# Two-layer network of graph convolutions and feed-forward parts: normalising stages and join unrolled with four slabs in flight, logits by token, weight preparation in stage tails, first scores ahead of the slab product

## What is computed

```python
x = x + _L0_conv_ref(_ln_c(x), ...)          # normalised over the 512 nodes
t = _to_tokens(x)                            # (16, 192, 512)
t = t + _L0_ffn_ref(_ln_t(t), ...)           # 8 experts, 2 for each token
x = _from_tokens(t, x)
x = x + _L1_conv_ref(_ln_c(x), ...)
t = _to_tokens(x)
t = t + _L1_ffn_ref(_ln_t(t), ...)           # quantised, up and down
```

## Time and profile before

| | us |
|---|---|
| median of 3 runs (1862.98 to 1868.24) | 1864.14 |
| the profiled execution's own time | 1862.88 |
| its span | 1861.1 |
| TensorE busy (matmul) | 1435.1 (77%) |
| VectorE busy | 1113.9 (60%) |
| ScalarE busy | 751.4 (40%) |
| GpSimd busy | 635.8 (34%) |

### The profile page before, as it was taken

How to read it: one execution, slowest core, us unless ns; L and a number is a source line. 1 busy time by engine, 2 the same in 40 slices (tenths; PEclk the granted TensorE clock), 3 DMA queues, 4 the chain that set the end, 5 groups by cost and what they waited for, 6 DMA issues and landing times. The chain is left out here.

```text
span 1861.1 us, 28248 instructions
## 1 busy us (share of the span) xinstructions
PE 1435.1 (77%) x8462; PEld 1179.6 (63%) x8462; DVE 1113.9 (60%) x2381; ACT 751.4 (40%) x1181; POOL 635.8 (34%) x918
## 2 busy tenths in 40 slices
PE   4578899999464289999999945497999994277676
PEld 4467788887343278888888834395888883155554
DVE  4622488888465654444445335313788886688886
ACT  2412455555242033333333224222555552177775
POOL 1100065556310446555555421000455565011111
PEclk7778899999697579999999965697999997588988
DMA  6423012221374046556555377343122121112221
GB/s 200 144 82 88 9 60 76 68 68 60 113 229 150 12 121 124 108 97 130 122 120 110 38 200 221 99 113 124 44 76 68 59 76 51 43 51 83 94 76 60
DMA packets 95966, 179.95 MB, mean 97 GB/s; under 512 B 13937, under 2 KB 31905, under 8 KB 95909
## 3 DMA queue, kind: packets, MB, share of 16 engines
q1 hardware_dynamic: 71828, 135.52, 23.1%
q0 software_dynamic: 16384, 31.51, 9.8%
q10 hardware_dynamic: 7696, 12.22, 2.1%
HBM read 113.12 MB, written 66.10 MB: 96 GB/s over the span
## 5 line engine op out<-in xcount | busy, mean ns | idle before, releaser
L731 PE MATMUL g_y<-L_z,L_pt 128*128 128x192 f32 x1024 | 197.5, 337 | 1.5 <-ACT L_pt L944 0.5
L889 POOL TENSOR_TENSOR L_xr<-L_xr,L_lnb 128x192 f32<-128x192 f32 x128 | 106.3, 859 | 208.1 <-DMA L_xr<-x 112.2
L731 PEld LDWEIGHTS g_y<-L_z,L_pt 128*128 128x128 f32 x1024 | 167.4, 194 | 6.8 <-ACT L_pt L944 6.8
L1269 POOL DMA_INDIRECT sums<-x_yo,x_places x64 | 103.0, 1609 | 136.4 <-ACT x_yo L1472 126.3
L936 ACT ACTIVATE L_e<-g_s,L_nm 128x512 f32<-128x512 f32 x128 | 88.0, 687 | 79.2 <-DVE L_nm L777 78.2
L699 PE MATMUL g_z<-L_kw,L_xnT 96*128 96x192 f32 x512 | 97.0, 344 | 26.1 <-DVE L_v L807 26.1
L699 PEld LDWEIGHTS g_z<-L_kw,L_xnT 96*128 96x128 f32 x512 | 87.1, 198 | 38.2 <-DVE L_v L807 38.2
L1381 DVE TENSOR_TENSOR x_mid<-ex_g,x_sig 128x480 f32<-128x480 f32 (+1 forms) x48 | 31.3, 653 | 132.8 <-ACT x_sig L1463 125.5
L896 POOL TENSOR_TENSOR L_t<-L_rstd 128x48 f32<-128x48 f32 x96 | 29.2, 305 | 224.5 <-DVE L_rstd L831 219.5
L777 DVE TENSOR_REDUCE L_nm<-g_s 128x1 f32<-128x512 f32 x128 | 87.5, 684 | 27.6 <-PE g_s L708 26.8
L786 DVE SCALAR_TENSOR_TENSOR L_p<-L_e,L_rl,L_adj 128x512 f32<-128x512 f32 x128 | 99.2, 775 | 4.7 <-DVE L_rl L784 0.3
(11 more groups left out here) (281 smaller groups left out, 3843.8 us busy)
## 6 DMA issues: line engine op xcount, KB each, us to landing
xn_rows<-L_xnT SPq DMA_DIRECT2D x48, 384.0 KB, 3.5
L_xnT<-xn_rows SPq DMA_DIRECT2D x48, 384.0 KB, 3.4
x<-L_y SPq DMA_DIRECT2D x32, 384.0 KB, 2.5
L_xa<-in_x SPq DMA_DIRECT2D x16, 384.0 KB, 3.9
L_raw<-xn_rows SPq DMA_DIRECT2D x16, 384.0 KB, 3.4
L_xr<-in_x SPq DMA_DIRECT2D x16, 384.0 KB, 3.4
L_xa<-x SPq DMA_DIRECT2D x16, 384.0 KB, 3.9
sums<-L_raw ACTq DMA_DIRECT2D x16, 384.0 KB, 3.1
```

The lines of the kernel that those rows point to most:

```text
L731: last = nc.tensor.matmul(out, pt[k % 2][:, P * c:P * c + P], z[q][:, c, :], start=False, stop=(c == NK - 1))
L889: last = nc.gpsimd.tensor_tensor(v_, v_, gain(s.lnb), ALU.add)
L1269: nc.gpsimd.indirect_dma_start(sums, row(places[e % 2][:, 1, t:t + 1]), yo[t % 4][:, :], None, compute_op=ALU.add).then_inc(sent[t % 4], 16)
```

## The change

- **Constants.** The block of constants goes. The identity is the first DMA of n0, then slabs 0 and 1, the other ten constants, slabs 2 and 3, then the 13 weight transfers, all on SP's queue. Only TensorE waits for the identity.
- **normalise** is written out slab by slab. Four slab buffers (xr0 and xr1 join xa), four buffers of normalised rows, three of raw rows; psx is three deep in n0, two deep in n1. Two BN_AGGR replace four of the small steps. In n0 ScalarE instead of VectorE copies the nodes; VectorE's list is shift(b-1), statistics(b). Stores are two DMAs of half a slab.
- **Logits** are made by token: eight products a slab with the nodes as the stationary side, [96, 8] each, kept in one PSUM bank and copied once at the end of n1. `route` loses its transposes and copy, and waits for its tables only ahead of the choice of experts (L1118).
- **conv_weights** becomes the tail of n0 and of the join: VectorE does it behind its last statistics (in the join behind its last copy), TensorE ahead of the last transposes back (n0) or at the end (join); GpSimd clears u and v there, and the clears leave `graph_conv`.
- **combine** is written out too, with three buffers of normalised rows and of node-major slabs; the weight transfers move from ScalarE's queue to SP's, the store of the node-major slab from SP's to ScalarE's.
- **graph_conv**: spread 2 goes ahead of scores 0 of the next slab, transposes 3 behind them, and the slab product behind both; `row_max(b + 1, 0)` goes ahead of `residual` and `variance`; ScalarE's `copy_turned(b, 2)` goes ahead of `row_exp(b, 3)`, and `copy_z` behind `row_exp(b + 1, 0)`.

```diff
--- normalise, SP
+                def load(b):
+                    since(sp, slab_turned, b - 3)
+                    sp.dma_start(xa[b % 4][:, :, :], src[b]).then_inc(xa_in[b % 4], 16)
+                if consts:
+                    consts.first(sp)
+                load(0)
+                load(1)
+                if consts:
+                    consts.rest(sp)
+                load(2)
+                load(3)
+                if prefetch:
+                    prefetch(sp)
+                for b in range(B):
+                    sp.wait_ge(xn_done, b + 1)
+                    for h in range(2):
+                        sp.dma_start(xn_rows[b][:, h, :], xn[b % 4][h]).then_inc(sent[b % 4], 16)
+                    if b + 4 < B:
+                        load(b + 4)
--- normalise, TensorE
+                def logits(b):
+                    pe.wait_ge(nodes_sb, b + 1)
+                    for h in range(2):
+                        at = E * (2 * b + h)
+                        for k in range(NK):
+                            last = nc.tensor.matmul(psl[0:HALF, at:at + E], na[b % 2][:, k, HALF * h:HALF * h + HALF],
+                                                    s.wr[:, k, :], start=(k == 0), stop=(k == NK - 1))
+                    last.then_inc(logits_done, 1)
+                for b in range(D):
+                    turn_slab(b)
+                for b in range(B):
+                    if tail and b == B - 1:
+                        tail.tensor(pe, psx[1])
+                    if route:
+                        if b + D < B:
+                            turn_slab(b + D)
+                        turn_back(b)
+                        since(pe, nodes_sb, b)
+                        if b > 0:
+                            logits(b - 1)
+                    else:
+                        turn_back(b)
+                        if b + D < B:
+                            turn_slab(b + D)
--- normalise, VectorE
+                for b in range(B + 2):
+                    if route and 0 <= b - 2 < B:
+                        copy_nodes(b - 2)
+                    if 0 <= b - 1 < B:
+                        take_shift(b - 1)
+                    if b < B:
+                        statistics(b)
+                if consts:
+                    consts.landed(dve)
+                if tail:
+                    tail.vector(dve, psx[1])
--- normalise, ScalarE
+                for b in range(B + 1):
+                    if route and b < B:
+                        keep_raw(b)
+                    if b < B:
+                        apply_norm(b)
+                    if route and b < B:
+                        send_raw(b)
+                    if not route and b > 0:
+                        copy_nodes(b - 1)
--- ConvWeights
+    def gpsimd(self):
+        for padded in (self.s.u0, self.s.u1, self.s.v0, self.s.v1):
+            self.nc.gpsimd.memset(padded[:, :].bitcast(F32), 0.0)
--- combine, SP and ScalarE
+                for b in range(4):
+                    load(b)
+                prefetch(sp)
+                for b in range(B):
+                    if b + 4 < B:
+                        load(b + 4)
+                    sp.wait_ge(xn_done, b + 1)
+                    for h in range(2):
+                        sp.dma_start(xn_rows[b][:, h, :], xn[b % 3][h]).then_inc(sent[b % 3], 16)
...
+                    act.wait_ge(x_sb, b + 1)
+                    act.dma_start(x_nodes[b], x2[b % 3][:, :, :]).then_inc(kept[b % 3], 16)
--- graph_conv, TensorE
+                    if k == 0:
+                        pe.wait_ge(uv_sb, ready(b))
                     pe.wait_ge(nmax_done, free(n, 2))
...
                         spread(b, q, 1)
+                        spread(b, q, 2)
+                    if project:
+                        scores(b + 1, r, 0)
+                    if softmax:
+                        turn_probs(b, 3)
                     if project:
                         conv_slab(b + 1, r)
-                        scores(b + 1, r, 0)
-                    if softmax:
-                        spread(b, q, 2)
-                        turn_probs(b, 3)
-                    if project:
                         scores(b + 1, r, 1)
--- graph_conv, VectorE
-                for padded in (*u, *v):
-                    nc.vector.memset(padded[:, :].bitcast(F32), 0.0)
...
                         row_probs(b, 3)
+                    if project:
+                        row_max(b + 1, 0)
                     if total:
                         residual(b - 2, q, i - q)
                     if norm:
                         variance(b - 1, r)
                     if project:
-                        row_max(b + 1, 0)
                         row_probs(b + 1, 0)
--- route
-                for j in range(TILES):
-                    last = nc.tensor.transpose(psl[0:HALF, E * j:E * j + E], s.logits[:, HALF * j:HALF * j + HALF],
-                                               s.ident[0:E, 0:E])
-                last.then_inc(logits_turned, 1)
```

550 lines of the change are left out of this document (253 added, 297 removed).

## The result

The kernel after takes 1849.64 us (median of 4 runs, 1849.0 to 1849.89) against 1864.12 before: ratio 0.9924, 95% interval 0.9902 to 0.9947. Forecast: 1820, range 1778 to 1852. The time lies just inside the range and the direction was right, the size was not: -14.5 instead of -44 us. The profiled span is 1847.8 us, 13.3 less than before.

What follows compares the result with a forecast made beforehand. Slab stages were taken as bound by hand-overs, graph convolution by nearly tied TensorE and VectorE-GpSimd cycles. Terms -33 - 15 - 3 - 24 - 7 + 39 = -43 took 1862.9 to 1820 us, range 1778 to 1852.

Steps and rivals of the forecast that it cites:

- The turn: Graph convolution, each slab: VectorE waits for late scores, so 16.9 us becomes 18.3; +39 us over 28 turns.
- The piece from the residual to the transposes of block 2: Graph convolution: VectorE and GpSimd chain from residual through Newton, divide and probabilities to TensorE's transposes; 13.18 us of the cycle.
- my slower rival: Graph convolution: TensorE idles 2 us a turn, so its clock drops to 1.2 GHz in part of the turns; 1900 us, chance 0.04.
- Routing: Transposes and a copy go, and the selection's first part no longer waits for the tables' DMA: -3 us.
- The first stage with the constants: Constants, first normalising stage and weight preparation: earlier start and 3.0 us a slab, small attention near 66 us: -33 us.
- Both graph convolutions with their starts: Both layers: turns +39 us; starts -7 us from moved clears and a shorter wait for the first probabilities.
- Newton runs bare: Graph convolution rival: GpSimd's Newton steps take 4.34 us, cycle 17.3, +11 instead of +39; 1792 us, chance 0.13.
- TensorE stays the bound: Graph convolution rival: VectorE's cycle hides, only the 0.61 us wait goes, -18 instead of +39; 1763 us, chance 0.13.
- the stage with logits: Second normalising stage: transfers set 4.0 us a slab instead of 5.17, products by token cost equal: -15 us.
- the hand-over of statistics, root and shift stays what paces them: Slab stages rival: hand-overs, or DMA engines losing rate, leave only half of the 72 us gain; 1856 us, chance 0.13.
- The join: Slabs paced by transfers at 3.7 us each, attention starting near 1165 instead of 1189.53: -24 us.
- slab 4 comes up to 4 us later: First stage and join: weights moved to SP's row stand in front of slab 4 instead of beside it; up to 4 us.

Runs made afterwards that it cites:

- experiment 2: Kernel after with only VectorE's first row maximum moved back behind residual and variance; TensorE's and ScalarE's new orders stay: 1789.63 us.
- experiment 3: Kernel after with TensorE's and ScalarE's graph convolution orders as before, VectorE's new order (row maximum ahead of residual and variance) kept: 1901.84 us.
- experiment 5: Kernel after with the old logits products (router weights stationary, four a slab), VectorE's copy per slab and the routing's transposes and copy back: 1829.84 us.
- the square above: Stage with logits alone, four kernels: copy ahead of shift, 77.9 us with old products, 95.1 by token; shift ahead of copy, 64.5 and 68.8 us.
- Experiment 8: Kernel after with the old logits products, and in addition VectorE's shift ahead of its copy in the stage with logits and the join: 1811.22 us.
- Experiment 10: Kernel after with the convolution's weights issued on ScalarE's queue, as before, instead of SyncE's, in the first stage and the join: 1847.84 us.
- experiment 1: Kernel after with TensorE, VectorE and ScalarE in their old graph convolution orders; the clears stay on GpSimd: 1811.08 us.

## Why the prediction was wrong

**Right in kind.** The turn: "18.5, and I take 18.3" against 18.17 in one turn and 19.42 in the next. VectorE idle ahead of the maximum, with residual and variance behind it, is in the rows and in experiments 2 and 3. The piece from the residual to the transposes of block 2, forecast 13.2 us, takes 13.7 and 13.0 in two turns in a row (from 317.05 and from 336.47). One link of the path was wrong: TensorE waits a step earlier than forecast, ahead of the projections, through ScalarE's list. The stretch at half clock was my slower rival's mechanism, at a fraction of its size. Routing: -3 forecast, -2.8 measured; the wait for the tables moved to L1203 as I wrote.

**Right by luck.** Two totals are right because misses cancel. The first stage with the constants: -33 forecast, -32.6 measured. But slab 4 was at TensorE at 23.86 us where I had 19.5, and the slabs behind it came 2.67 us apart (statistics from 25.84 to 55.26 over eleven of them) where I had 3.0: 4.4 us lost and 3.6 gained. Both graph convolutions with their starts: +32 forecast, +34 measured. But the turns, from the first division to the last, cost 24.6 us a layer and so 49 instead of 39, 18.84 us a turn on average over the first thirteen; and the starts gained 15 instead of 7. Of that gain 12.3 us lie between the first Kronecker product and the first division (57.3 us before in either layer, 50.9 and 51.5 after), where TensorE's wait of 2.35 us for the first probabilities is gone; ahead of the Kronecker product the first layer gained 3.3 us and the second lost 0.5.

**Rivals that fell.** Newton took 5.34 us (from the end of L924 at 319.62 to the division at 324.96), and 4.33 where VectorE only waits, so the rival "Newton runs bare" fell. By the rule of the Trainium skill (GPSIMD Engine Reference, Specifications) it was to stay slow beside VectorE's instructions with two SBUF inputs, and the trace agrees: the three slow steps of the twelve, 0.61, 0.43 and 0.82 us against 0.27 to 0.29, lie beside L879, L887 and L879, and the step beside the maximum, which reads PSUM, takes 0.28. The rival "TensorE stays the bound" fell too, though experiment 2 shows the gain that it spoke of, 0.5 us a turn, behind VectorE's move.

**The step that failed** is the stage with logits, -15 forecast, +3.9 measured with the gap before it: "1.18 MB, at 218/0.74 = 295 GB/s are 4.0 us, more than any engine needs", and of the products by token "between free and twice as dear, 0 and 3 us a slab less or more, I take equal". Slabs came 4.8 to 5.8 us apart. The sum took the pace as the largest of the lists, and the pace was a ring through four engines, closed by one place in VectorE's list: copy ahead of shift. The ring gives 4.35 us at full clock, which alone would have missed little: with the old products and the ring (experiment 5) the stage takes 12.8 us less than before. The products by token in that ring were granted half the clock, which makes the ring up to 5.8 us and TensorE's own list as long (1.91 + 1.49 + 2.62 us a slab, the last in the row below). That is 17.3 us for a term that I took as nothing, and 4.3 where the ring is open. So the transfers were not the pace, and the products were not equal; either error mended alone takes the stage more than 12 us under the 90.7 of before, by the square above. Experiment 8 shows that the forecast of a DMA-paced stage comes true, and more, once the ring is open. Why the clock is low with the new products in the ring, and full with either changed, no run shows. My rival "the hand-over of statistics, root and shift stays what paces them" named the kind of cause, with 0.13; the half of 72 us that it gave up would have been 1856, measured is 1850, though the first stage gave its whole gain.

```profile
517.94 2.62 PE L392 MATMUL n_psl<-s_wr,L_sqr 128*96 128x8 f32 x16
```

**The join**, -24 forecast, -16.1 measured, is the ring alone, at a smaller size: TensorE's clock is 0.50 in it before and after. The ring in the middle of the stage, from shift to shift:

```profile
1110.84 0.15 DVE L308 SCALAR_TENSOR_TENSOR L_nm<-L_mv,L_rs 96x2 f32<-96x2 f32 x1
1111.02 1.52 ACT L1689 ACTIVATE L_xnT<-L_p,L_nm,L_rs 96x512 f32<-96x512 f32 x2 [2.00 <-DVE L_nm L308]
1112.59 1.54 PE L1659 MATMUL join_a<-s_ident,L_xnT 96*128 96x96 f32 x8 [1.39 <-ACT L_xnT L1689]
...
1114.17 0.96 DVE L1632 COPY L_shared<-join_a 128x768 f32<-128x768 f32 x1 [1.51 <-PE join_a L1659]
1115.05 0.15 DVE L308 SCALAR_TENSOR_TENSOR L_nm<-L_mv,L_rs 96x2 f32<-96x2 f32 x1
```

4.21 us where I had 3.7 by bytes. Opened, the join takes 7.7 us less (experiment 8), which is the 8 that were missing.

By the rule of the Trainium skill that each DMA engine takes turns between the rows of its issuing engines (DMA: Bandwidth & Descriptors, queues, rings and completion order) I had estimated that slab 4 comes up to 4 us later. Experiment 10 gives 0.6 us for slab 4, and shows the sharing in slab 2, which comes 6.8 us later when the weights are beside it.

The misses: 19 in the stage with logits, 8 in the join, 2 in the graph convolutions (10 in the turns less 8 in the starts), which is the 29 us between -43 and -14.

## What to carry to other kernels

A stage that is spread over several engines has a ring as well as lists: follow one item from an instruction to the next item's same instruction, through every wait for data and for a buffer, and only then call it bound by its transfers. In such a ring the order of two small calls on one engine is worth much: here 0.15 us of shift behind 0.96 us of copy cost 32 us, where the whole change without its reorder had gained 53 (experiment 1). And before an instruction is moved ahead, look at what stands behind it on its engine: the move pays only if its operand is already there; a change that bundles a gain and such a move shows neither until they are run apart. The same goes for causes that work on each other: neither the ring nor the new products alone explains 95.1 us, only the square of four runs does. And a total that comes out right is no proof of its terms; compare each of them with the trace.

## What the runs showed of the hardware

- TensorE's granted clock in the stage with logits followed neither the ring nor the form of the product alone: in the ring it was, in mid-stage, 1.00 with the old products and with twice as many of them, 0.59 to 0.66 with the products by token and 0.50 to 0.67 with a quarter of these; off the ring it was 1.00 with either form. A half clock lengthens the ring from 4.35 to 5.82 us, since TensorE's two groups of transposes lie in it (1.91 and 1.49 us instead of 1.05 and 0.83).
- In the graph convolution, stretches at half clock (0.66 in a window of 5 us) stood right behind a wait of TensorE of 1.7 to 1.8 us, but only in every other turn for the most part; with the orders of before (experiment 1), where no such wait is, there is none from 200 to 430 us.
- The DMA engines moved 335 GB/s at a share of 0.99 in the stage with one load and two stores a slab (experiment 8), where 218 GB/s at 0.74 had given an estimate of 295.
- The two BN_AGGR instructions that had no row before take 0.18 and 0.15 us each (L296, L297), near the small step, as taken.
